# Attention block on one core: rows of batches 1 to 7 normalised by ScalarE as factor and addend, not by VectorE

## The reference

```python
xn = _layernorm(x, axis=-1)                      # (x - m) / sqrt(v + 1e-5)
x = x + attn(xn, ...) + ffn(xn, ..., ln_g, ln_b)
# in attn:
mu = mean(x); var = mean((x - mu) ** 2)
xn = (x - mu) * rsqrt(var + LN_EPS) * norm_g + norm_b
q = xn @ Wq;  k, v = split(x @ Wkv)
q = l2norm(q) * q_scale;  k = l2norm(k) * k_scale
sim = q k^T * 8 - slope * |distance|, causal
out = softmax(sim) v ;  return out @ Wout
```

## Time and profile before

| | us |
|---|---|
| median of 3 runs | 2789.91 (2785.57 to 2790.7) |
| profiled execution, whole time | 2793.3 |
| its span, first to last instruction | 2791.3 |
| PE busy | 2646.4 |
| VectorE busy | 2555.2 |
| ScalarE busy | 2132.3 |
| GpSimd busy | 2174.8 |
| mean granted TensorE clock | 0.987 of full speed |

### The profile page before, as it was taken

One profiled execution on the slowest core, in us unless ns is written; L12 is line 12 of the kernel. 1 busy time (PEld: TensorE's weight loads), 2 busy tenths in 40 slices (PEclk: granted clock), 3 DMA queues, 4 the chain that ended last, 5 costly groups with the idle time before them and its releaser, 6 DMA issues. The chain is left out here.

```text
span 2791.3 us, 84780 instructions
## 1 busy us (share of the span) xinstructions
PE 2646.4 (95%) x31631; PEld 1570.5 (56%) x31631; DVE 2555.2 (92%) x6760; ACT 2132.3 (76%) x3385; POOL 2174.8 (78%) x2438
## 2 busy tenths in 40 slices
PE   5689999999999999999999999999999999999997
PEld 3355555555555555555655555555555555555554
DVE  7799999999999999999989999999999999899996
ACT  5477787777777788777877778877777777777775
POOL 6696878877788687977879778897778868798663
PEclk7899999999999999999999999999999999999999
DMA  5222354423533244434443235433354333542222
GB/s 185 42 49 52 72 102 87 82 64 71 95 104 69 61 75 92 108 60 67 89 89 95 52 75 101 86 88 59 69 102 97 69 69 69 89 103 55 50 50 65
DMA packets 629574, 220.17 MB, mean 79 GB/s; under 512 B 593584, under 2 KB 595632, under 8 KB 629168
## 3 DMA queue, kind: packets, MB, share of 16 engines
q1 hardware_dynamic: 627696, 214.67, 37.4%
q10 hardware_dynamic: 1472, 0.09, 0.0%
HBM read 55.23 MB, written 16.78 MB: 26 GB/s over the span
## 5 line engine op out<-in xcount | busy, mean ns | idle before, releaser
L1027 DVE CUSTOM_DVE_ANT_0 PS<-PS,STR 128x512 f32<-128x512 f32 (+3 forms) x1536 | 822.3, 580 | 82.1 <-PE PS L1275 72.9
L589 ACT ACTIVATE AR<-PS,SC 128x1024 f32<-128x1024 f32 (+1 forms) x640 | 653.6, 1021 | 164.8 <-PE PS L1286 100.4
L1228 PE MATMUL PS<-WH,XT 128*128 128x388 f16 x2048 | 680.2, 332 | 38.2 <-DVE AR L1040 31.4
L1230 PE MATMUL PS<-WH,XT 128*128 128x388 f16 x2048 | 677.9, 331 | 0.0
L1229 PE MATMUL PS<-WL,XT 128*128 128x388 f16 x2048 | 677.4, 331 | 0.0
L593 ACT ACTIVATE AR<-AR 128x1024 f16<-128x1024 f32 (+1 forms) x640 | 621.8, 972 | 20.3
L799 POOL TENSOR_TENSOR RN<-SS,HALF 128x8 f32<-128x8 f32 x256 | 450.4, 1760 | 165.8 <-DVE SS L1112 163.9
L1068 DVE TENSOR_TENSOR AR<-AR 128x768 f16<-128x768 f32 (+1 forms) x448 | 546.6, 1231 | 9.4 <-ACT AR L593 9.0
L1251 PE MATMUL PS<-AR 64*128 64x512 f16 (+3 forms) x4608 | 496.2, 324 | 19.9 <-ACT AR L589 19.4
L1313 PE MATMUL PS<-AR 128*128 128x66 f16 x4608 | 474.4, 196 | 3.2 <-DVE AR L1068 1.9
L1315 PE MATMUL PS<-AR 128*128 128x64 f16 x4608 | 470.3, 192 | 0.0
(11 more groups left out here) (221 smaller groups left out, 5210.8 us busy)
## 6 DMA issues: line engine op xcount, KB each, us to landing
XW<-in_L_attn_x SPq DMA_DIRECT2D x112, 256.0 KB, 3.0
out<-ACC SPq DMA_DIRECT2D x64, 256.0 KB, 2.2
ACC<-in_L_attn_x SPq DMA_DIRECT2D x56, 256.0 KB, 2.9
AR<-QKB SPq DMA_TRANSPOSE x512, 2.5
AR<-in_L_attn_Wkv SPq DMA_DIRECT2D x2, 1536.0 KB, 12.5
ACC<-in_L_attn_x SPq DMA_DIRECT2D x2, 1024.0 KB, 7.3
AR<-in_L_attn_Wout SPq DMA_DIRECT2D x1, 2048.0 KB, 9.3
AR<-CTK SPq DMA_TRANSPOSE x128, 2.4
```

Source lines behind the costliest of these rows:

```text
L589: e.activation(PR[:, n % 2, :, 0:wide], SB[:, :, 0:wide], ACT.Exp, scale=SIG).then_inc(s_p, 1)
L1027: e.tensor_tensor_reduce(out=r[:, 0:n], in0=r[:, 0:n], in1=ST[:, u % 2, h, o:o + n], scale=1.0, scalar=LOW, op0=ALU.add, op1=ALU.max, accu ...
L1228: e.matmul(PJ, XT[:, k, xs], WH[:, k, p, :], start=k == 0, stop=False)
L1230: ins = e.matmul(PJ, XT[:, 4 + k, xs], WH[:, k, p, :], start=False, stop=k == KC - 1)
```

## The change

For batches 1 to 7 the norm of a row tile, 56 in all, moves from VectorE to ScalarE. It is written there as factor times x plus addend, with a new row 5 of RX as the addend (row 4 times 64), which GpSimd computes with one more instruction per batch at the end of `ln_small`. The count of `s_rx` goes from 11 to 12 per batch. The slots are those of before: the tables are kept. Within a slot ScalarE's new step stands right ahead of the high halves. Batch 0 keeps VectorE's form.

```diff
-        RX = sb("RX", [P, 2, 5, NT], F32)
+        RX = sb("RX", [P, 2, 6, NT], F32)
...
+                for b, t in due_ln(s, W_XF):
+                    w.wait_ge(s_rx, 12 * (b + 1))
+                    w.wait_ge(s_x[t % 2], 16 * (NT * (b - 1) + 4 + t // 2 + 1))
+                    e.activation(XW[:, t % 2, :], XW[:, t % 2, :], ACT.Identity, bias=RX[:, b % 2, 5, t:t + 1],
+                                 scale=RX[:, b % 2, 2, t:t + 1]).then_inc(s_xf, 1)
                 for b, t in due_ln(s, W_XH):
                     ln_hi(b, t)
...
                     e.tensor_scalar(R[:, 2, :], R[:, 1, :], XS, None, ALU.mult).then_inc(s_rx, 1)
                     w.wait_ge(s_rx, n + 2)
+                    e.tensor_scalar(R[:, 5, :], R[:, 4, :], XS, None, ALU.mult).then_inc(s_rx, 1)
+                    w.wait_ge(s_rx, n + 3)
...
-                for b, t in due_ln(s, W_XF):
-                    ln_xf(b, t)
```

More of the change, by code:

```diff
@@ L635, in _ @@
                         w.wait_ge(s_xin[t // 4], 16)
-                    w.wait_ge(s_rx, 11 * (b + 1))
+                    w.wait_ge(s_rx, 12 * (b + 1))
                     w.wait_ge(s_base, 3 * i)
@@ L677, in ln_small @@
                 mean, var = MV[:, b % 2, :, 0], MV[:, b % 2, :, 1]
-                n = 11 * b + (0, 2, 5, 6, 9)[part]
+                n = 12 * b + (0, 2, 5, 6, 9)[part]
                 if part == 0:
@@ L914, in ln_xf @@
             def ln_xf(b, t):
[L915 to L918, removed]
+                w.wait_ge(s_rx, 12 * (b + 1))
+                if t > 1:
                     w.wait_ge(s_xl, t - 1)
-                e.tensor_scalar(XW[:, t % 2, :], XW[:, t % 2, :] if b else ACC[:, t, :], MV[:, b % 2, t, 0:1], RX[:, b % 2, 2, t:t + 1],
+                e.tensor_scalar(XW[:, t % 2, :], ACC[:, t, :], MV[:, b % 2, t, 0:1], RX[:, b % 2, 2, t:t + 1],
                                 ALU.subtract, ALU.mult).then_inc(s_xf, 1)
```

## The result

The changed kernel takes 2795.27 us (median; 2790.68 to 2803.2), the kernel before, on the same chip, 2789.48 (2781.0 to 2793.52). The ratio is 1.0027, with a 95% interval of 1.0018 to 1.0037: slower by 7.5 us, 5.0 to 10.3. The prediction had the direction and a sum of 11.2 us. The profiled execution of the changed kernel is its fastest, 2790.7 us, at a granted clock of 0.991 where the one before had 0.987. So the two spans are not compared as a whole, but place by place.

The account below looks back on a forecast made before the run. The prediction took PE as the bound, VectorE close behind; 3.8 (tile 1) + 2.5 (tile 3) + 4.9 (tile 7) = 11.2 us on a median of 2789.9 gave 2801.1 us, range 2790 to 2815.

Parts of the forecast that it names:

- The bound and the relief: PE bounds the kernel; VectorE's norms cost PE nothing, so taking them away wins nothing there.
- fourth case: Rival, chance 0.07: relief of VectorE and less contention with GpSimd outweigh the delays; faster, 2785 us.
- the rule beside it: GpSimd and VectorE contend for SBUF interfaces, so the move would relieve both engines at 56 places.
- The price of the step: On ScalarE each norm lasts 806 ns, 0.71 us of its time; no table load; GpSimd 0.23 us per batch.
- Tiles 0, 2, 4, 5, 6 at nothing: These norms on ScalarE cost nothing, falling into idle time or harmless places; bounds 0.2 us earlier, 0.7 us later.
- Tile 1, 6 x 0.63: Norm ahead of an exponential makes PE wait 0.63 us for scores in six batches: 3.8 us.
- Tile 3, 7 x 0.35: Norm delays eviction L560 by 0.35 us, lengthening PE's row maximum wait in seven batches: 2.5 us.
- Tile 7, 4 x 0.7 + 2.1: ScalarE waits for XW's load, delaying PE: 0.7 us in four batches, 2.1 in batch 4; total 4.9 us.
- The sum: Tiles 1, 3 and 7 together: 3.8 + 2.5 + 4.9 = 11.2 us slower, median 2801.1 us.
- The signs to look for: Expected in the changed profile: ScalarE waits for XW's load; longer waits for L560, L589, L1027 and L1040; VectorE's busy time 40 us lower.
- second case: Rival, chance 0.20: the wait at tile 7 is paid in full, 1.5 us more per batch; about 2811 us.
- third: Rival, chance 0.18: PE's new waits replace later ones, leaving one long load at tile 7; 2792 us.

Follow-up runs that it names:

- none: Changed kernel with the norm of batches 1 to 7 left out on both engines, the high half reading raw rows; ratio 1.0003 to the kernel before.
- on_v_137: Changed kernel, but the norms of tiles 1, 3 and 7 stay on VectorE, 35 norms go to ScalarE; ratio 1.0001 to the kernel before.
- only1: Kernel before with only tile 1's norm moved to ScalarE, the other seven staying on VectorE; ratio 1.0003 to the kernel before.
- slots127: Changed kernel with tiles 1 and 2 moved to slot -26 and tile 7 to slot 22; ratio 1.0003 to the kernel before.
- slots12: Changed kernel with the norms of tiles 1 and 2 moved to slot -26, behind the exponential; ratio 1.0019 to the kernel before.
- slot7: Changed kernel with tile 7's norm three slots later, 22 in place of 19; ratio 1.0024 to the kernel before.
- buf7: Changed kernel with tile 7's second load going to a buffer of its own; ratio 1.0018 to the kernel before.
- only7: Kernel before with only tile 7's norm moved to ScalarE, tiles 0 to 6 staying on VectorE; ratio 1.0024 to the kernel before.
- slots_all: Changed kernel with tiles 1 and 2 at slot -26, tile 3's norm and both halves at 0, tile 7 at 22; ratio 1.007 to the kernel before.
- slots_fix: As slots_all, with tile 5's norm also moved from slot 6 to 10; ratio 1.0079 to the kernel before.

## Why the prediction was right, and where its sum was too large

**The bound and the relief: right.** VectorE's norms were predicted to cost PE nothing. none shows it: 1.0003. With it falls the fourth case (faster), and the gain that the rule beside it would give: the Trainium skill, "GPSIMD Engine Reference", section "8. Key points", on GpSimd and VectorE contending for SBUF. Lines with 533 and 1261 ns for the same form may come from that, but removing all 56 is worth nothing here beyond the 2 us that the interval leaves open.

**The price of the step: right.** 804 ns against 806, 0.71 us of queue time, no table load, 0.23 us on GpSimd. VectorE's busy time fell by 31 us, not 40: its other instructions took 9 us more.

**Tiles 0, 2, 4, 5, 6 at nothing: right** within what can be told (on_v_137, 1.0001, with 0.2 us in a last unit).

**Tile 1, 6 x 0.63: right in size.** only1 has 0.64 us per unit. PE's wait in batch 4 is 0.45 us, though, not 0.6; the rest shows as 0.2 us more of busy time in the same unit. The count of six was read from one profile: ahead of batch 2 PE had waited 0.98 us for a transpose, which the prediction took for a property of the batch. In after this wait is absent, and PE waits 0.33 us for the exponential there; the unit is 41.20 us before and 41.21 after. Ahead of batch 7, too, little was added (40.47 to 40.72 us), since PE was held there already. So five units grew by tile 1 between the two profiles. But in after PE has this wait ahead of six batches (not ahead of batch 1), 0.33 to 0.46 us, and in only1 six units, all but the one ahead of batch 2, are 0.64 us longer: that the prediction left out one batch of seven did not make its sum too large.

**Tile 3, 7 x 0.35: right**, 0.31 to 0.32 us.

**Tile 7, 4 x 0.7 + 2.1: the term that was mis-sized, in three of its batches.** The chain is the predicted one up to PE's wait for L1040. Its last link, VectorE's lag that makes PE's next pieces 0.4 us late, does not show: PE's wait for the row maximum at the end of batch 4's first unit is 0.78 us, in slots127 it is 0.79. In batches 2 to 5 the first units are 0.63, 0.43, 0.62 and 1.09 us above 42.51, 0.69 on average. Two steps failed. The 2.1 us took the one load of 4.5 us, which batch 4 had in the profile before, as a property of that batch; in after it landed in 2.7 us and cost 0.6. And batches 6 and 7 were put at nothing, since ScalarE came to the place 2.4 us behind the issue, where it was 1.2 to 1.4 us in the others. That too belonged to the profile: in these two PE had waited 1.10 us for a transpose some 6 us ahead of the load's issue. In slots12, where PE has no such wait, ScalarE is at the place 1.56 us behind the issue in all seven batches; it waits 1.08 and 1.33 us for the load in batches 6 and 7, against 0.98 to 1.11 in the others, and their first units are 0.63 and 0.82 us above 42.51. Batch 7, before (PE), then in slots12 (ScalarE, PE):

```profile
2398.16 0.38 PE L1328 MATMUL PS<-WO,OT 128*128 128x512 f16 x1 [1.10 <-DMA OT<-OTK]
...
2407.67 0.81 ACT L609 ACTIVATE XW<-XW,RX 128x512 f32<-128x512 f32 x1 [1.33 <-DMA XW<-in_L_attn_x]
...
2411.72 0.33 PE L1231 MATMUL PS<-WH,XT 128*128 128x388 f16 x1 [0.44 <-DVE AR L1045]
```

Over seven batches tile 7 costs 301.9 - 7 x 42.51 = 4.3 us in slots12, and 5.3 to 5.7 us by the first units of after against slot7 and buf7. That the term's total of 4.9 is close to this is luck: against slots12 it has 1.5 us too many in batch 4 and 1.5 too few in batches 6 and 7 together. A lone long load, or a lone wait next to a place, in one profile is no term of a sum, but a part of the range.

**The sum.** By units that nothing else disturbs the three places would cost 7 x 0.64 + 7 x 0.32 + 4.3 = 11.0 us, about the predicted 11.2. The ratio gives 7.5 (5.0 to 10.3), the units against none 9.9. Between the two profiles the seven last units are 285.6 - 280.5 = 5.1 us longer, the seven first ones 304.3 - 301.8 = 2.5, together 7.6. The rest is missing where PE was held by something else in before: in the first units of batch 1 (44.02 us before, 43.43 after) and batch 6 (43.67 and 43.66) and in the last units ahead of batches 2 and 7. There the profiles show a new wait in the place of another. The prediction had this only as a bound of tile 1, and its sum has no term for it. How often it happens in executions that were not profiled, and what sets those other waits, no run shows.

**The signs to look for.** VectorE's wait for L560 grew by 23.7 us (10 or more were expected), PE's for L589 by 3.4 (4), ScalarE waited for the load in each batch, 0.7 to 1.5 us (1 to 4 were expected in batches 1 to 5, and less after; batch 7 has 0.95 as batch 3 has). PE's wait for the row maximum grew by 4.6 (2 expected). That for L1040 grew by only 0.8 in all (3 to 4 expected), although it is there in batches 2, 4 and 5 with 0.25, 0.23 and 0.63 us, and in only7 the total is 35.8 us in 26 waits, 4.4 more than before. What the first unit of batch 4 lost beyond the 0.2 us shows as PE's busy time, 42.06 us against 41.72 in slots127, and not in the later wait on which the prediction had put it.

**The rivals.** The second case (tile 7 in full, 0.7 + 1.5 us per batch) is out by only7, which has 1.0 us. The third (no change) is out by the interval's lower end, 1.0018, though only just: PE does not get back what it loses at tiles 1 and 3.

## What to carry to other kernels

A step that moves to another engine takes its waits along, and whatever is queued behind it there pays them; so, where a table of slots is kept, look first whether the new engine comes to that slot earlier than the step's data does. Relief of an engine is worth only what the bound engine waits for it, and leaving the step out altogether shows that ceiling before any place is tuned. A price read from one profile holds only for the waits that this profile happens to have. Steps that hand on a buffer form a chain (here load, norm, halves, transpose, next load), and moving one link later can hold a queue far from it, as slots_all and slots_fix show.

## What was not expected of the hardware

A long wait of PE can cost more than its own length. In slots_all PE idles 3.43 us in the first unit of batch 4; its granted clock then falls to the lower of its two levels (1.2 GHz, half of the full 2.4) for part of the time:

```profile
1394.55:1402.00 7.45, 7.39 (x88) 4.45 (x84) 4.34 (x15) 3.47 (x7) 4.27 (x6) 1.00 0.60 62
1402.00:1405.43 3.43, 0.00 (x0) 0.00 (x2) 0.81 (x1) 2.77 (x5) 1.29 (x2) 1.00 0.64 141
1405.43:1408.00 2.57, 2.57 (x32) 1.56 (x33) 2.57 (x6) 2.57 (x5) 2.49 (x3) 0.67 0.69 151
1408.00:1410.00 2.00, 2.00 (x27) 1.19 (x24) 1.97 (x7) 1.77 (x3) 1.38 (x2) 0.57 1.06 219
1410.00:1412.00 2.00, 2.00 (x12) 0.80 (x9) 1.51 (x3) 1.81 (x3) 1.10 (x1) 1.00 0.56 112
```

The column behind GpSimd's is the clock: 1.00 up to the wait and through it, 0.67 and 0.57 in the 4.6 us behind it, 1.00 again from 1410. The same unit one batch later, with a wait of 1.79 us at this place, keeps the clock at 1.00:

```profile
1394.55:1442.13 47.58, 43.30 (x505) 25.54 (x502) 37.35 (x105) 36.26 (x59) 32.52 (x37) 0.96 0.54 101
1731.10:1778.11 47.01, 42.05 (x504) 24.71 (x501) 37.33 (x103) 36.24 (x59) 32.20 (x37) 1.00 0.55 102
```

PE is busy for 43.30 us against 42.05, so the lower clock costs 1.25 us on top of the wait. In slots_fix the first six matmuls behind the wait of 4.02 us take 1.46 us, against 0.82 in the row of slots_all. The waits of 0.2 to 0.9 us which the change itself makes leave the clock at 1.00 in their units. The length of one wait alone does not tell, though: elsewhere in the same profile the clock is at 0.52 behind a wait of 1.93 us, which is hardly longer than the 1.79 us above.

```profile
1184.22 0.84 PE L1254 MATMUL PS<-AR 64*128 64x512 f16 x4 [1.93 <-ACT AR L589]
...
1184.50:1188.00 3.50, 3.50 (x52) 2.58 (x49) 3.35 (x6) 3.06 (x6) 3.16 (x5) 0.52 0.46 80
```
